# Causal products of GpSimd over two successive pairs of heads at once, with new order lists on four engines: a post-norm layer on one core

## The chip, the cores and the metric

The kernel runs on one core of a Trainium2 chip. The metric is device time in microseconds (us) of one execution. Five engines work side by side, each through its own queue in order: PE (matmul, with PEld for its weight loads), DVE (vector), ACT (activation), POOL (GpSimd) and SP (which issues the transfers). They meet only at semaphores.

## The reference, cut to what matters

For each of 16 batches of 512 rows by 128 columns: causal attention with 16 heads of 8 columns (q and k normalised, scores capped by tanh), a layer norm, then a routed block: a router picks 63 rows of each batch, which go through an attention and a feed-forward of their own and are scattered back, then a second layer norm.

```python
    def _L0_attn_ref(x, w_q, w_k, w_v, w_o):
        ...
        scores = jnp.einsum('bhqd,bhkd->bhqk', q, k) / jnp.sqrt(jnp.float32(dk))
        scores = jnp.tanh(scores / SOFTCAP) * SOFTCAP
        causal = jnp.tril(jnp.ones((S, S), dtype=bool))
        scores = jnp.where(causal[None, None], scores, -jnp.inf)
        probs = jax.nn.softmax(scores, axis=-1)
        y = jnp.einsum('bhqk,bhkd->bhqd', probs, v)
        ...
    x = L0_attn_x
    x = _layernorm(x + _L0_attn_ref(x, ...), axis=-1)
    x = _layernorm(x + _L0_ffn_ref(x, ...), axis=-1)
```

## The kernel before, in words

**The attention.** Heads are worked two at a time, so a batch has eight pairs of heads (`gi` 0 to 7; `n` counts them over all batches, 128 in all). For each pair of heads PE forms the scores with the keys on the partitions, in eight blocks of 64 keys, the causal lower part only, 2304 columns in two units (L1172, `ps_s`). ACT takes the tanh of each unit (L710, `th`) and then the exp of all 2304 columns (L725, `pr`). On the diagonal of each of the eight blocks 64 columns have to be multiplied by the triangle `tri`: `causal` on POOL (L621) does that in two instructions for each pair of heads, five blocks (320 elements a partition) and three (192). `pr` has five buffers of 2304 columns, from the 48th pair of heads on six (`probs_at`). PE's steps pv.0 to pv.3 then multiply four pairs of heads by the values (L1189), pv.4 to pv.7 the other four; the first of each four waits for the semaphore `masked`.

**The stages of a batch.** "prep" makes q, k and v (transposes, `qk0`, `qk1`, `v` on PE; the squares `sq` on POOL, sums and an inverse root on DVE, then `hi` on DVE and `lo` on POOL, L635, which split q and k into two 16-bit parts). "fin" takes the attention's output through its projection (`wo`, `res`), the layer norm (`ln`, `root1`, `root2`) and `x1`. "route" finds the chosen rows: `xw` on POOL, `w`, `row`, four comparisons `win` (L936, `wins`), `rank`, `coef`. Then, for two batches together, "sel" gathers the chosen rows and their mask (`xs`, `ss`, roots, `hn`, `hnT`, `qkv`, `qkT`, `R`, `RT`, `msel`), "att" is the routed block (`S0`, `S1` on PE, `sc0`, `mx0`, `sc1`, `mx1`, `den`, `PT0`, `PT1`, `o`, `oT`, `x1f`, roots, `h`, `hh`, `hp`, `hu`, `g`), and "late" scatters back (`proc`, `z0`, `z1`, POOL's `z_base`) and does the last layer norm (`ln`, `root1`, `root2`, `norm`). Steps called `root1` and `root2` are three or four DVE instructions each on tiny tiles (L798 to L808), an inverse root by a polynomial; moments (L883 to L893) are bn_stats and five small steps.

**What sets the order.** Four tables written out by hand: `PE_ORDER`, `VE_ORDER` (DVE), `POOL_ORDER` and `ACT_ORDER`; SP has a fixed list. An iteration `p` takes two batches (0 and 1) through 16 steps of two halves; in each half an engine runs the entries of its table, `name/k@shift`, where k is the batch of the two and the shift says by how many iterations the work lags. Scores, tanh, exp and the causal products stand in the loops themselves. Nothing but semaphores ties the halves of two engines to each other, so a table sets an order, not a time. `BANK` says which of two PSUM banks a step of PE uses, `BANK_READ` whose reading it must await.

Of the kernel before, what the change touches and what calls it, by code (L numbers as in the profile page):

```python
# [61 lines left out]
def moments_of(tiles, tag=""):  # L62
# [45 lines left out]
    [], ["prep.qk1/1@0", "att.S0@-2"],  # L108
    ["att.S1@-2", "pv.4/1@-1", "pv.5/1@-1", "route.thr/1@-2"], ["pv.6/1@-1", "pv.7/1@-1"],
    ["prep.v/1@0"], ["att.P0@-2", "att.P1@-2"],  # L110
    [], ["att.PV@-2"],
    [], ["fin.wo/1@-1", "att.oT@-2"],
    ["pv.0/0@0", "pv.1/0@0", "pv.2/0@0"], ["att.wo@-2", "pv.3/0@0", "prep.xT/0@1"],
    [], ["route.wrow/0@-1", "prep.qk0/0@1"],
    ["att.h2T@-2"], ["att.w1@-2"],
    ["route.won/0@-1"], ["prep.qk1/0@1", "route.wrow/1@-1"],
    ["pv.4/0@0", "pv.5/0@0"], ["pv.6/0@0", "pv.7/0@0"],
    ["route.thr/0@-1", "route.won/1@-1"], ["late.w2@-2", "prep.v/0@1"],
    [], ["sel.gather@-1", "sel.gather1@-1", "late.sc0@-2"],
    ["late.sc1@-2"], ["fin.wo/0@0"],  # L120
    ["pv.0/1@0", "pv.1/1@0", "sel.ET@-1", "pv.2/1@0"], [],
    ["sel.hnT@-1", "pv.3/1@0", "sel.R@-1", "sel.qkv@-1"],
    ["sel.R1@-1", "sel.R2@-1", "sel.qkT@-1", "sel.R3@-1", "prep.xT/1@1"],
# [4 lines left out]
    ["prep.qk0/1@0", "sel.msel@-2", "late.ln@-3", "prep.qk1/1@0"], ["att.sc0@-2"],  # L128
    ["att.mx0@-2", "att.sc1@-2", "att.mx1@-2", "fin.x1/0@-1"], ["route.coef/1@-2", "att.den@-2", "prep.v/1@0"],
    ["att.PT0@-2", "fin.yU1/1@-1", "prep.ss/1@0"], ["att.PT1@-2"],  # L130
# [1310 lines left out]
```

## Time and profile before

| | |
|---|---|
| median of 3 runs | 839.63 us (839.16 to 841.62) |
| profiled execution | 842.9 us, span 841.1 us |
| PE busy | 676.7 us, 80% of the span |
| DVE busy | 664.8 us, 79% |
| ACT busy | 555.4 us, 66% |
| POOL busy | 391.0 us, 46% |

The span is the time between the first and the last instruction of the profiled execution. A share of busy time is a mean over the whole of it: at the start ACT, later other engines have little left, and the end is a chain for the last two batches alone. So the rows below go by stretches. An instruction's duration in the trace runs from its start on the engine to its end, and may contain time in which it stands still.

### The profile page before, as it was taken

The numbers are of one execution on the slowest core, as the hardware profiler recorded it, in microseconds if no ns is written. First come the engines' busy times: TensorE is split into PE (matmuls) and PEld (weight loads), VectorE is DVE, ScalarE is ACT, GpSimd is POOL, SyncE is SP. The second block draws the span as 40 slices with busy tenths as digits, with TensorE's granted clock in tenths as the row PEclk, the third lists the DMA queues.
The fourth block names the chain that finished last, engine by engine and source line by source line (L and its number), as shares of the span: only waits on it lengthen the run. The fifth ranks groups of instructions, "written<-read, shape, count | busy, mean of one in ns | idle before, by whom it ended". The sixth has DMA issues, their size and how long they took to land.

```text
span 841.1 us, 16526 instructions
## 1 busy us (share of the span) xinstructions
PE 676.7 (80%) x6384; PEld 391.2 (47%) x6384; DVE 664.8 (79%) x1649; ACT 555.4 (66%) x403; POOL 391.0 (46%) x399
## 2 busy tenths in 40 slices
PE   3578787889898998888788988989789889973852
PEld 2334444535554455645454455545464546442432
DVE  3631849688979899879997899889988998588456
ACT  0388898978886778768784778688866888600000
POOL 5262645456554474455553464545635554421201
PEclk9557777889787977898896977897988978865855
DMA  6311203033303212130403012120303030000001
GB/s 188 63 34 43 55 23 76 2 63 115 76 2 63 64 22 56 39 63 2 76 28 63 14 37 53 45 46 2 64 26 64 1 64 27 13 1 26 0 1 50
DMA packets 97855, 36.72 MB, mean 44 GB/s; under 512 B 69090, under 2 KB 95090, under 8 KB 97778
## 3 DMA queue, kind: packets, MB, share of 16 engines
q1 hardware_dynamic: 97778, 35.67, 18.7%
q8 instruction: 51, 0.84, 0.4%
q14 instruction: 26, 0.21, 0.1%
HBM read 14.69 MB, written 4.19 MB: 22 GB/s over the span
## 4 chain that ended last, share of the span: by engine, by line
DVE 43%; PE 40%; issue 8%; ACT 6%; DMA 1%; POOL 1%; SPq 0%; DVEq 0%; ACTq 0%
PE ps_y L1189 10%; PE ps_s L1172 8%; PE ps_m L1288 4%; DVE wins L936 4%; ACT pr L725 3%; ACT th L710 2%; PE ps_a L1220 2%; DVE qn_v L844 2%; PE ps_m L1228 2%; DVE st L854 2%; DVE sel_v L803 2%; PE ps_a L1238 2%; DVE sel_v L802 2%; DVE v_aug L838 2%; PE ps_m L1389 1%
## 5 line engine op out<-in xcount | busy, mean ns | idle before, releaser
L710 ACT ACTIVATE th<-ps_s 128x1024 f32<-128x1024 f32 (+1 forms) x256 | 281.9, 1129 | 140.8 <-PE ps_s L1172 130.8
L621 POOL TENSOR_TENSOR pr<-pr,tri 128x320 f32<-128x320 f32 (+1 forms) x256 | 194.4, 781 | 190.3 <-ACT pr L725 190.2
L725 ACT ACTIVATE pr<-th 128x2304 f32<-128x2304 f32 x128 | 271.4, 2121 | 9.8 <-PE ps_y L1189 9.6
L1172 PE MATMUL ps_s<-q_st,k_st 32*64 32x192 f16 (+7 forms) x2048 | 197.4, 329 | 31.7 <-ACT th L710 24.3
L1189 PE MATMUL ps_y<-pr,v_aug 128*32 128x512 f32 (+7 forms) x2048 | 167.0, 470 | 0.7 <-POOL pr L621 0.7
L1172 PEld LDWEIGHTS ps_s<-q_st,k_st 32*64 32x64 f16 x2048 | 93.9, 117 | 124.6 <-issue 43.9
L1189 PEld LDWEIGHTS ps_y<-pr,v_aug 128*32 128x32 f32 x2048 | 62.5, 120 | 90.1 <-issue 74.3
L635 POOL TENSOR_TENSOR st<-qk,st 128x1024 f16<-128x1024 f32 x32 | 73.2, 2307 | 59.5 <-DVE st L854 59.5
L623 POOL TENSOR_TENSOR k_wide<-qkT,head_of 128x1024 f32<-128x1024 f32 x16 | 30.1, 1901 | 52.6 <-DVE qkT L1019 52.6
L936 DVE SCALAR_TENSOR_TENSOR wins<-w_wide,x,later 128x512 f16<-128x512 f32 (+1 forms) x64 | 48.1, 751 | 1.9
L623 POOL TENSOR_TENSOR z_base<-x,coef 128x512 f32<-128x512 f32 x16 | 16.6, 1040 | 55.0 <-DVE coef L960 55.0
L623 POOL TENSOR_TENSOR st<-qk 128x1024 f32<-128x1024 f32 x16 | 30.7, 1917 | 19.2 <-DVE qk L827 19.2
L692 ACT ACTIVATE pm<-pm 128x1008 f32<-128x1008 f32 x8 | 8.3, 1037 | 42.5 <-DVE pm L1033 42.5
L1288 PE MATMUL ps_m<-mask_a,E 128*64 128x512 f32 x112 | 36.0, 666 | 0.3 <-DVE y_out L1104 0.3
L862 DVE STREAM_TRANSPOSE y_u<-ps_y 128x512 f32<-128x512 f32 x32 | 22.8, 712 | 16.4 <-PE ps_y L1189 16.3
L1350 PE MATMUL ps_m<-vv,k_wide 128*128 128x32 f32 x128 | 26.1, 376 | 11.7 <-DVE k_wide L1045 11.7
L696 ACT ACTIVATE sc<-hu 128x512 f32<-128x512 f32 x8 | 5.0, 624 | 44.3 <-POOL hu L623 44.3
L838 DVE COPY v_aug<-ps_m 64x512 f32<-64x512 f32 x32 | 22.0, 686 | 14.7 <-PE ps_m L1228 14.2
L1238 PE MATMUL ps_a<-wT,yT 128*128 128x128 f32 x128 | 32.3, 431 | 0.0
L1350 PEld LDWEIGHTS ps_m<-vv,k_wide 128*128 128x128 f32 x128 | 25.3, 302 | 13.5 <-DVE k_wide L1045 13.5
L1238 PEld LDWEIGHTS ps_a<-wT,yT 128*128 128x128 f32 x128 | 27.7, 319 | 4.8 <-issue 4.0
L623 POOL TENSOR_TENSOR r<-x,rw_row 128x512 f32<-128x512 f32 x16 | 21.1, 1321 | 14.2 <-DVE x L912 14.2
(221 smaller groups left out, 1114.0 us busy)
## 6 DMA issues: line engine op xcount, KB each, us to landing
x_in<-in_L_attn_x SPq DMA_DIRECT2D x16, 256.0 KB, 3.4
x_res<-in_L_attn_x SPq DMA_DIRECT2D x16, 256.0 KB, 3.4
result<-y_out SPq DMA_DIRECT2D x16, 256.0 KB, 2.2
mask_a<-in_L_ffn_attention_mask SPq DMA_DIRECT2D x3, 1024.0 KB, 5.2
pr<-in_L_ffn_attention_mask SPq DMA_DIRECT2D x2, 1024.0 KB, 8.4
w_sb<-in_L_ffn_w SPq DMA_DIRECT2D x2, 256.0 KB
q_st<-st SPq DMA_TRANSPOSE x16, 4.5
k_st<-st SPq DMA_TRANSPOSE x16, 4.8
```

The source lines that it names most:

```text
L621: return nc.gpsimd.tensor_tensor(buf, buf, tri[:, None, :].to_broadcast([P, blocks, 64]), ALU.mult)
L623: mul = lambda out, a, b: nc.gpsimd.tensor_tensor(out, a, b, ALU.mult)
L635: pl["prep"].done(nc.gpsimd.tensor_tensor(lo_parts[s], qk_twice[s], hi_parts[s], ALU.subtract), f"lo_{part}", b)
L710: nc.scalar.activation(th[:, gi % 2, c0:c1], ps_s[:, c0:c1], ACT.Tanh, scale=1.0 / (QK_SCALE ** 2 * DH ** 0.5 * SOFTCAP))\
L725: nc.scalar.activation(pr[:, probs_at(n):probs_at(n) + GROUP], th[:, gi % 2, :], ACT.Exp, scale=SOFTCAP).then_inc(exp_done, 1)
L838: ve["prep"].done(nc.vector.tensor_copy(v_aug[rows, k].rearrange("p b n c -> p (b n) c")[:, :, 16 * s:16 * s + DH], at("prep.v", b)[rows, ...
L936: step(lambda: nc.vector.scalar_tensor_tensor(won[c], w_wide[:, P * c:], x1[:, k, c, D:D + 1], later[:, 0:n], ALU.is_le, ALU.mult, accum_o ...
L1172: last = mm(ps_s[64 * s:64 * s + 64, COL[kb]:COL[kb] + S - 64 * kb], k_st[rows, k, gi // 2, 64 * kb:64 * kb + 64], q_st[rows, k, gi // 2, ...
L1189: last = mm(ps_y[32 * j:32 * j + 32, 64 * kb:S], v_aug[:, k, kb, gi, :], pr[:, c:c + S - 64 * kb], start=(kb == 0), stop=(kb == NB - 1), s ...
L1238: last = mm(at("fin.wo", b)[:, P * c:P * c + P], yT[:, P * c:P * c + P], wT[:, 3, :], start=True, stop=True)
L1288: last = mm(at("sel.R")[SLOTS * k:SLOTS * k + SLOTS, :], E[:, c, SLOTS * k:SLOTS * k + SLOTS], (mask_b if k and q < 2 else mask_a)[:, c, : ...
L1350: last = mm(at("att.PV")[:, 32 * n:32 * n + 32], PT[:, n, :], vv[:, n, :, :].rearrange("p k c -> p (k c)"), start=True, stop=True)
```

## The change

`causal` now works on two successive pairs of heads, n and n + 1 with n even, in one instruction: an access pattern with one more dimension of two buffers. In place of four instructions (320, 192, 320, 192 elements) there are two (640 and 384). POOL does this at the odd pair of heads, after that one's exp, and counts `masked` once. PE waits for half as many counts. The four tables are laid anew, and with them the banks. In `VE_STEPS`, "hn" and "ET" of "sel" change places.

```diff
-            def causal(n, col, step, blocks):
-                buf = pr[:, probs_at(n) + col:probs_at(n) + col + step * blocks]\
-                    .rearrange("p (n c) -> p n c", c=step)[:, :, 0:64]
-                return nc.gpsimd.tensor_tensor(buf, buf, tri[:, None, :].to_broadcast([P, blocks, 64]), ALU.mult)
+            def causal(n, first, step, blocks):
+                lo, hi = sorted((probs_at(n) // GROUP, probs_at(n + 1) // GROUP))
+                buf = pr[:, 0:6 * GROUP].rearrange("p (g n c) -> p g n c", g=6, c=64)[
+                    :, lo:hi + 1:hi - lo, first:first + step * (blocks - 1) + 1:step, :]
+                return nc.gpsimd.tensor_tensor(buf, buf, tri[:, None, None, :].to_broadcast([P, 2, blocks, 64]), ALU.mult)
...
-                        pool.wait_ge(exp_done, b.no * 8 + (gi + 1))
-                        causal(b.no * 8 + gi, 0, 512, 5)
-                        causal(b.no * 8 + gi, 960, 448, 3).then_inc(masked, 1)
+                        if gi % 2:
+                            pool.wait_ge(exp_done, b.no * 8 + (gi + 1))
+                            causal(b.no * 8 + gi - 1, 0, 8, 5)
+                            causal(b.no * 8 + gi - 1, 15, 7, 3).then_inc(masked, 1)
...
-                    t_.wait_ge(masked, b.no * 8 + (4 * half + 4))
+                    t_.wait_ge(masked, b.no * 4 + (2 * half + 2))
...
-    ["sel.RT@-1"], ["prep.qk0/1@1", "sel.msel@-1"],
+    [], ["sel.RT@-1", "prep.qk0/1@1"],
```

In POOL's table the steps move too. Before, `sel.zb` (z_base) and `prep.sq/1` stood in the first half of an iteration and `route.xw/0` in the eighth; now the three follow each other in the third. `att.kw` (k_wide) now comes directly behind `prep.lo/0`; before, two pairs of heads stood between. In the changed file the lines of these parts stand one or two lower.

On DVE, in the middle of the program, behind the two casts of prep.hi for an even batch (`st<-qk`; `sel_v` is the tile of sel.root1, `y_out<-ps_m` is late.z1, `hnT` sel.hnT). Before:

```order
L854 CAST st<-qk 128x64x16
L854 CAST st<-qk 128x128x8
L800 TENSOR_SCALAR sel_v<-sel_v 128x1
L802 TENSOR_TENSOR sel_v<-sel_v 128x1
L803 TENSOR_TENSOR sel_v<-sel_v 128x1
L805 SCALAR_TENSOR_TENSOR sel_v<-sel_v 128x1
```

After:

```order
L855 CAST st<-qk 128x64x16
L855 CAST st<-qk 128x128x8
L1105 TENSOR_TENSOR y_out<-ps_m,z_base 128x512
L979 COPY ET<-ps_a 128x512
L995 TENSOR_SCALAR hnT<-ps_m,g 128x256
L884 BN_STATS stats<-y_out 128x6 x8
L887 TENSOR_TENSOR mv<-stats 128x8
```

sel.root1 and sel.root2 now stand ahead of the casts; late.z1 and late.ln have come behind them.

On DVE, behind the two casts of prep.hi for an odd batch (`x<-r` is route.w, `r<-ps_a` fin.res; `w_wide` is route.row). Before:

```order
L854 CAST st<-qk 128x64x16
L854 CAST st<-qk 128x128x8
L920 TENSOR_REDUCE x<-r 128x4
L921 TENSOR_SCALAR x<-x,rb 128x4
L901 TENSOR_TENSOR r<-ps_a,x_res 128x512
```

After:

```order
L855 CAST st<-qk 128x64x16
L855 CAST st<-qk 128x128x8
L930 COPY w_wide<-ps_a 128x512
L878 STREAM_TRANSPOSE yT<-y_n 128x512
L1059 COPY oT<-ps_m 128x128
L937 SCALAR_TENSOR_TENSOR wins,cnt<-w_wide,x,later 128x512
```

route.row and route.win of the even batch now follow the casts, and route.w stands earlier.

On DVE, from the copy of R (`w_wide<-ps_m`) to att.sc0 (`sc`). Before:

```order
L980 COPY w_wide<-ps_m 128x512
L822 COPY xT<-ps_a 128x512
L992 COPY RT<-ps_m 128x512
L805 SCALAR_TENSOR_TENSOR ln_v<-ln_v 128x4
L806 SCALAR_TENSOR_TENSOR ln_v<-ln_v 128x4
L807 SCALAR_TENSOR_TENSOR ln_v<-ln_v 128x4
L808 SCALAR_TENSOR_TENSOR ln_v<-ln_v 128x4
L827 COPY qk<-ps_a 128x8x64
L1018 COPY msel<-ps_m 128x64
L883 BN_STATS stats<-y_out 128x6 x8
L886 TENSOR_TENSOR mv<-stats 128x8
```

After:

```order
L981 COPY w_wide<-ps_m 128x512
L823 COPY xT<-ps_a 128x512
L863 STREAM_TRANSPOSE y_u<-ps_y 128x512
L993 COPY RT<-ps_a 128x512
L828 COPY qk<-ps_m 128x8x64
L1019 COPY msel<-ps_a 128x64
L1027 SCALAR_TENSOR_TENSOR sc<-ps_m,msel 128x512
L1033 TENSOR_REDUCE mx<-sc 128x8
L1034 TENSOR_TENSOR pm<-sc,mx 128x8x63
L828 COPY qk<-ps_m 128x8x64
```

att.sc0 now follows msel at once; fin.root2 and late.ln, which stood between the copy of RT and att.sc0, are elsewhere, and qk1/1 has moved behind att.mx0. On PE the same place reads, after the change (`w_wide` transposed is RT, `wT,xT` is qk0/1, `E,RT` is msel, `k_wide,qkT` is S0):

```order
L1197 MATMUL ps_a<-ident,w_wide 128x128 x4
L1221 MATMUL ps_m<-wT,xT 128x8x32 x2
L1173 MATMUL ps_s<-q_st,k_st 64x512 x2
L1173 MATMUL ps_s<-q_st,k_st 64x448 x2
L1173 MATMUL ps_s<-q_st,k_st 64x64 x2
L1321 MATMUL ps_a<-E,RT 64x64 x8
L1337 MATMUL ps_m<-k_wide,qkT 64x512 x2
```

Before, S0 stood behind another unit of scores and qk1/1; msel came directly behind qk0/1.

## Rows read from the trace of the kernel before

**Rows 1.** Busy time of each engine by stretch, then clock, DMA share, GB/s.

```profile
40.00:196.80 156.80, 130.34 (x1278) 66.70 (x1277) 97.90 (x199) 134.81 (x97) 80.77 (x81) 0.75 0.24 54
473.90:563.90 90.00, 80.06 (x801) 46.32 (x801) 82.68 (x204) 69.02 (x52) 47.83 (x47) 0.85 0.19 42
196.80:742.00 545.20, 478.23 (x4716) 276.60 (x4714) 481.06 (x1187) 410.07 (x297) 280.53 (x274) 0.84 0.18 39
742.00:841.10 99.10, 51.37 (x306) 36.97 (x298) 66.23 (x220) 3.35 (x4) 13.74 (x11) 0.62 0.06 17
```

**Rows 2.** DVE's waits, 473.9 to 563.9 us: first and last of seven; total, times, longest.

```profile
DVE r L901 <- PE ps_a L1238: 1.1, 1, 1.1
...
DVE w_wide L929 <- PE ps_m L1196: 0.3, 1, 0.3
```

**Rows 3.** Timeline, 540.3 to 547.5 us: start, duration, instruction.

```profile
541.17 4.60 POOL L635 TENSOR_TENSOR st<-qk,st 128x1024 f16<-128x1024 f32 x2 [5.15 <-DVE st L854]
...
541.79 1.90 DVE L802 TENSOR_TENSOR sel_v<-sel_v 128x1 f32<-128x1 f32 x1
...
543.73 2.05 DVE L803 TENSOR_TENSOR sel_v<-sel_v 128x1 f32<-128x1 f32 x1
```

**Rows 4.** Single lines over the whole run: shortest, median, longest in ns.

```profile
L802 DVE TENSOR_TENSOR sel_v<-sel_v x16: 158/360/1909, 174.8 to 814.8; 128x1 f32<-128x1 f32 x16
L870 DVE TENSOR_TENSOR y_n<-y_u,rd x16: 691/774/1877, 87.8 to 749.6; 128x512 f32<-128x512 f32 x16
L886 DVE TENSOR_TENSOR mv<-stats x24: 164/348/1200, 98.6 to 834.0; 128x4 f32<-128x4 f32 x16, 128x8 f32<-128x8 f32 x8
L921 DVE TENSOR_SCALAR x<-x,rb x16: 231/517/1391, 136.2 to 766.7; 128x4 f32<-128x4 f32 x16
```

**Rows 5.** Timeline of DVE: the first, one and the last of the long ones.

```profile
488.60 0.86 DVE L870 TENSOR_TENSOR y_n<-y_u,rd 128x512 f32<-128x512 f32 x1
...
498.48 1.38 DVE L921 TENSOR_SCALAR x<-x,rb 128x4 f32<-128x4 f32 x1
...
563.27 0.99 DVE L886 TENSOR_TENSOR mv<-stats 128x8 f32<-128x8 f32 x1
```

**Rows 6.** Groups by form, whole run: busy us, mean ns, idle before.

```profile
L621 POOL TENSOR_TENSOR pr<-pr,tri 128x320 f32<-128x320 f32 x128 | 115.4, 902 | 190.3 <-ACT pr L725 190.2
...
L621 POOL TENSOR_TENSOR pr<-pr,tri 128x192 f32<-128x192 f32 x128 | 84.4, 660 | 0.0
```

**Rows 7.** Groups by form of POOL, 473.9 to 563.9 us.

```profile
L635 POOL TENSOR_TENSOR st<-qk,st 128x1024 f16<-128x1024 f32 x4 | 9.2, 2319 | 8.6 <-DVE st L854 8.6
L623 POOL TENSOR_TENSOR st<-qk 128x1024 f32<-128x1024 f32 x2 | 3.8, 1892 | 0.0
...
L623 POOL TENSOR_TENSOR z_base<-x,coef 128x512 f32<-128x512 f32 x3 | 3.1, 1041 | 7.2 <-DVE coef L960 7.2
...
L623 POOL TENSOR_TENSOR sc<-hb 128x512 f32<-128x512 f32 x1 | 1.0, 1039 | 2.0 <-DVE hb L1081 2.0
```

**Rows 8.** Groups by form of DVE, 473.9 to 563.9 us.

```profile
L844 DVE TENSOR_REDUCE qn_v<-st 128x128 f32<-128x1024 f32 x2 | 2.4, 1196 | 0.0
...
L883 DVE BATCH_NORM_STATS2 stats<-y_out 128x6 f32<-128x128 f32 x8 | 1.6, 276 | 0.0
...
L978 DVE COPY ET<-ps_a 128x512 f32<-128x512 f32 x1 | 0.7, 691 | 0.0
```

**Rows 9.** Timeline of PE, 554.5 to 566.7 us.

```profile
558.38 1.13 PE L1220 MATMUL ps_a<-wT,xT 128*128 128x256 f32 x4
559.44 0.97 PE L1320 MATMUL ps_m<-E,RT 128*64 128x64 f32 x16
...
562.86 1.08 PE L1336 MATMUL ps_a<-k_wide,qkT 128*64 128x512 f32 x4
563.87 0.62 PE L1172 MATMUL ps_s<-q_st,k_st 32*64 32x512 f16 x6
```

**Rows 10.** ACT's waits, 40 to 200 us: total, times, longest.

```profile
ACT pr L725 <- PE ps_y L1189: 5.5, 5, 1.6
```

More of the change, by code:

```diff
@@ L107 @@
 PE_ORDER = (
[L108 to L123, printed above, removed]
-    ["sel.RT@-1"], ["prep.qk0/1@1", "sel.msel@-1"],
+    ["sel.msel@-2", "att.S0@-2"], ["att.S1@-2", "prep.qk1/1@0"],
+    ["pv.4/1@-1", "pv.5/1@-1", "route.thr/1@-2"], ["pv.6/1@-1", "pv.7/1@-1", "prep.v/1@0"],
@@ L125 @@
+    ["late.sc0@-2", "late.sc1@-2"], ["sel.ET@-1", "pv.0/1@0", "pv.1/1@0"],
+    ["pv.2/1@0", "pv.3/1@0", "sel.hnT@-1"], ["sel.R@-1", "sel.qkv@-1"],
+    [], ["sel.R1@-1", "sel.R2@-1", "sel.qkT@-1", "sel.R3@-1", "prep.xT/1@1"],
+    [], ["sel.RT@-1", "prep.qk0/1@1"],
 )
 VE_ORDER = (
[L128 to L130 removed]
@@ L138 @@
-    ["route.row/1@-1"], ["prep.qk1/0@1", "route.win/1@-1"],
-    ["late.norm@-3", "att.g@-2", "route.coef/0@-1"], ["route.rank/1@-1", "fin.yU1/0@0"],
-    ["prep.v/0@1", "late.proc@-2", "fin.y/0@0"],
-    ["prep.ss/0@1", "prep.root1/0@1", "fin.yT/0@0", "sel.xs@-1", "late.z0@-2"],
-    ["prep.root2/0@1", "sel.ss@-1", "prep.qkn/0@1"], ["fin.res/0@0", "prep.hi/0@1", "sel.root1@-1"],
-    ["sel.root2@-1", "sel.ET@-1"], ["sel.hn@-1", "late.z1@-2"],
-    ["sel.hnT@-1", "fin.ln/0@0", "fin.yU0/1@0", "sel.qkv@-1", "fin.root1/0@0"], ["sel.qkT@-1", "sel.R@-1"],
@@ new lines @@
+    ["prep.qk0/0@1"], ["att.hn@-2", "late.root1@-3", "fin.x1/1@-1", "att.h2T@-2"],
+    ["route.coef/0@-1", "fin.yU0/0@0", "route.w/1@-1"],
+    ["att.h@-2", "late.root2@-3", "att.hp@-2", "route.row/1@-1", "route.win/1@-1", "late.norm@-3", "att.g@-2", "prep.qk1/0@1"],
+    ["prep.v/0@1", "fin.yU1/0@0", "late.proc@-2", "route.rank/1@-1"], ["fin.y/0@0", "fin.yT/0@0", "sel.xs@-1"],
+    ["sel.ss@-1", "sel.root1@-1"], ["prep.ss/0@1", "fin.res/0@0", "late.z0@-2", "prep.root1/0@1", "prep.root2/0@1"],
@@ L146 @@
+    ["sel.root2@-1", "prep.qkn/0@1"], ["sel.hn@-1"],
+    [], ["prep.hi/0@1", "late.z1@-2", "sel.ET@-1"],
+    ["sel.hnT@-1", "late.ln@-2", "sel.qkv@-1"], ["fin.ln/0@0"],
+    [], ["sel.qkT@-1", "sel.R@-1"],
+    ["prep.xT/1@1", "fin.yU0/1@0", "sel.RT@-1"], ["prep.qk0/1@1", "sel.msel@-1", "att.sc0@-1"],
+    ["att.mx0@-1", "prep.qk1/1@1"], ["att.sc1@-1", "fin.root1/0@0", "att.mx1@-1"],
 )
 POOL_ORDER = (
-    ["sel.zb@-2", "prep.sq/1@0"], [],
+    [], [],
+    ["sel.zb@-2", "prep.sq/1@0", "route.xw/0@-1"], [],
@@ L251 @@
[L251 to L261 removed]
+    "att.PV": ["att.PT0@0"],
+    "att.S0": ["prep.qk0/1@2", "sel.R@0"],
```

134 lines of the change are left out of this document (70 added, 64 removed), and 2 rows, old and new, of the table VE_STEPS.

## The prediction

> **What bounds the kernel now.** I read the busy time by stretch first [rows 1]. From 196.8 to 742 us the batches flow through in pairs, six pairs in 545.2 us, of 92 us each but for the last; call one such turn a period. In the period from 473.9 to 563.9 DVE is busy 82.7 of 90.0 us, PE 80.1, ACT 69.0, POOL 47.8. The table of waits for the same period says which of the two full engines waits for which: DVE waits seven times, 4.0 us together [rows 2]; the rest of its 7.3 us without work is gaps between one instruction and the next. So DVE sets the pace here, and a microsecond more or less in its queue is a microsecond of the period. The stretch before (40 to 196.8) is another kind: ACT is busy 134.8 of 156.8 us, DVE 97.9. In the tail (742 to 841.1) nothing is full: it is one chain of dependent steps.
>
> The reader is to see next that DVE's busy time is not all work. At 541.17 POOL begins the two subtractions of prep.lo, 4.60 us; DVE's multiplications of a single element then take 1.90 and 2.05 us and end as POOL's two instructions do [rows 3]. The same form takes 0.16 us when it is quick [rows 4]. I went through the period and set each DVE instruction that starts under a running POOL instruction against the shortest of its own form and size: 29 are longer by over 0.06 us, 16.6 us together, from y_n at 488.60 (0.86 for 0.69) to the first moment step at 563.27 (0.99 for 0.16) [rows 4, 5]. Twenty of them stand behind causal products, 8.0 us (4.7 behind the wide ones, 3.3 behind the narrow ones, sixteen of each); nine behind other POOL work, 8.6 us, of which prep.lo alone makes 5.0. The 29 have two inputs in SBUF or are tensor_scalar steps from SBUF to SBUF; copies out of PSUM, transposes, reductions and bn_stats are never among them. Below, "open" steps are those of the 29's kinds.
>
> The Trainium skill says this in "SBUF — State Buffer", section "Who interferes with whom": VectorE and GpSimd share one port pair, which is an exclusive lock for a whole instruction, and DVE wants it for an instruction with two SBUF inputs and for some single-input forms. The trace agrees, at 1.90 us for one element.
>
> **The change, part by part.**
>
> *The products.* A period has 16 pairs of instructions, 0.90 us (320 elements) and 0.66 us (192) on the mean [rows 6]. The straight line through both is 0.30 us plus 1.89 ns an element, so 640 elements take 1.51 and 384 take 1.02. Eight times 2.53 us is 20.3 against sixteen times 1.56, 25.0. If nothing of the 0.30 is fixed it stays 25.0. POOL itself has over 42 us to spare in a period, so its saving is worth nothing by itself; what counts is how long DVE stands behind it. Today a product of 0.90 us costs DVE 4.7/16 = 0.295 us and one of 0.66 costs 3.3/16 = 0.205. On that line (0.37 us more per us of product) the merged ones cost 0.52 and 0.34, eight times that is 6.9 us, 1.1 less than now. If every additional us is waited out (DVE has an open step ready all the while), they cost 0.90 and 0.42, 10.5 us, 2.5 more than now. I take 0.2 less: nearer to the measured line, but not on it, since DVE comes to an open step the more surely the longer a product goes on. Bounds: -1.1 and +2.5.
>
> The page's rule by itself speaks against the merge: the loser is blocked to the end of the instruction, so an instruction twice as long blocks longer. By its worst case the sum would be the +2.5.
>
> *What DVE does behind the other POOL work.* This is the larger term, and the order lists decide it. Lengths of POOL work from [rows 7], of cover from [rows 8].
> - After prep.hi of the even batch DVE now goes to three quick copies and the eight bn_stats of late.ln, instead of sel.root1. prep.lo lasts 2 x 2.32 = 4.6 us from the end of hi_q. Cover: hi_k 0.6, z1 and ET 0.69 each, hnT some 0.5, bn_stats 1.6, together 4.1. Left: 0.5, against 3.64 now (1.90 + 2.05 - 2 x 0.16).
> - After prep.hi of the odd batch: copy and transpose of 0.69 each, oT some 0.3, then route.win, which is open. Cover with hi_k 2.2 of 4.6, left 2.4, against 1.34 now (L921 1.38 for 0.23 [rows 4, 5], and a first moment step 0.19). This one gets worse.
> - After route.coef/1 POOL does z_base twice (2.1), the squares (1.9) and xw/0 (1.0 to 1.4): 5.0 to 5.4 us. DVE has den and ss (1.2 each) and four copies (2.8): 5.2. Left about 0; now z_base and an xw cost 0.82 and 0.88.
> - xw/1 no longer falls on route.win: some 0.5, now 0.79. k_wide is covered by copies: 0, now 0.80. hh now meets late.root2 at once: 1.0, now 0.28; hu then meets win/1: 0.6, now 0.
>
> Together 5.0 us for 8.6: -3.6. The bounds are -5 (all covered) and -1 (the odd batch's loss stays, half of the rest comes back as POOL's queue shifts).
>
> *New waits of DVE for PE.* PE's steps have moved too. DVE now goes from the copy of RT through qk0/1 and msel straight to att.sc0; before, late.ln and qk1/1 stood between. PE meanwhile has qk0/1 (1.13), half a score group (0.62), msel (0.97) and S0 (1.08) [rows 9]. Laid out from the moment at which DVE starts to copy R, each DVE copy at 0.6 from start to start: DVE copies R, xT, y_u and RT until 2.4; PE has transposed RT by 1.3, is through qk0/1 at 2.4, the scores at 3.1, msel at 4.0, S0 at 5.1, then half a score group, S1 and qk1/1 until 8.2. DVE is ready for msel at 3.1, for sc0 at 4.2 and, after sc0, mx0 and sub0, for qk1/1 at 7.3: waits of 1.0, 1.1 and 0.9, together 3.0. The present waits in this region (qkT, R, RT) are 1.6 of the 4.0 [rows 2]; two of them get cover from fin.ln/0 and yU0/1. Others laid out in the same way: den and PT1 0.7, res/1 0.5, xs 0.7 (the gather is behind rank/1 with only y/0 and yT/0 between), h, proc and rank/0 0.3 each. Sum 5.8 against 4.0: +1.8. Bounds 0 (PE is ahead) and +5.6 (the four steps run at the lower clock level, 3.8 us more; the granted clock of the period is 0.85).
>
> *The mask later.* The first of a pair now waits for the second exp, and the pair's last product ends about 2.5 us after that exp, not 1.56. PE's pv waits for it, and exp waits for pv where five buffers are all there are. In the stretch where ACT is full, exp has waited five times, 5.5 us [rows 10]: up to 1.0 us is added to each, and to three more halves perhaps. I take +4 (bounds 0 and +8). Later ACT has 21 us a period to spare and it costs nothing; without that cover it would be 4 us a period.
>
> *The tail.* late.ln of the last pair but one moves ahead, behind qkv's round trip to PE, instead of standing in front of att.sc0 of the last pair: 2.5 us off the chain, of which I take 2 (bounds 0 and 4).
>
> **Sum.** A period: -3.6 - 0.2 + 1.8 = -2.0. 545.2 us hold 5.9 periods: -11.8. With +4 and -2: -9.8 us. The profiled execution took 842.9 us (span 841.1 and 1.8 around it), which gives 833.1; it is 3.3 over the median of the runs, 839.6, which gives 829.8. I say 830.
>
> **Rivals.**
> - *Larger gain.* Waits stay at 4.0 and the products follow the line: -4.7 a period, -27.7, with the ends -25.7: 814 us. For it: PE has 10 us a period free. Against: the ladder from RT to sc0 is a true dependency.
> - *No change.* Waits eat what the lock gives back: within 0.3%, 837 to 842 (0.3% is about what a measurement of this kernel can tell).
> - *Longer hold, slower.* The merged products each stop a chain of small two-input steps (roots, moments, win) for their whole length: +2.5 in place of -0.2, a period +0.7, in all +6: 846. It decides from the point where DVE stands 9.5 us a period behind products, not 8.0 (-3.6 + 1.5 + 1.8, and the +2 of the two ends spread over 5.9 periods). This is the page's rule as a result of its own; for it, the chain at 541 us, where two long instructions were waited out nearly whole; against it, the line of today's two lengths.
> - *The ladder, slower.* PE's four steps late or at the lower clock: +5.6 in place of +1.8, a period +1.8, in all +13: 852. It decides from 3.5 us more waits a period.
>
> **Chances.** Forecast (3 to 15 us gained) 0.38, larger gain 0.20, no change 0.13, longer hold 0.15, ladder 0.14. So faster 0.58, same 0.13, slower 0.29. The range takes in the larger gain a little beyond its time and the ladder: 808 to 853. Cases of both signs hold much of the chance; the forecast's own range is 824 to 837.
>
> **What would show it.** Right: periods of about 90 us; single-element steps of sel.root1 at 0.16 us throughout; products of about 1.5 and 1.0 us; DVE still busy over 85% with waits of 5 to 6 us a period, the largest before msel, sc0 and qk1/1; the first win of the odd batch long. Wrong: products of 1.8 us and more; small two-input steps of 1 to 1.5 us in rows behind the products; DVE's waits for S0 or msel over 2 us each; or exp waiting for pv past 200 us.

## The result, and the profile after

The changed kernel takes 809.57 us (median of four runs, 798.82 to 812.37) against 839.57 before; the medians stand at 0.964. The 95% interval of the ratio, 0.9467 to 0.9664 around 0.9566, is taken over the two runs within 1.5% of the fastest, 798.82 and 808.17. The forecast was 830: the sign is right and the median lies in the range of 808 to 853, near its lower end, but the gain is 30 us and not 10. The profiled run took 810.97 us; a later series of the same kernel gave 806.64 to 808.21 (median 807.20, against 838.54 before), so I read its profile as the usual case.

The busy time by stretch, of the kernel after; the stretches answer to those of [rows 1]: ACT-full start, one full period, the middle, the tail.

```profile
41.70:203.20 161.50, 130.38 (x1280) 65.38 (x1280) 93.06 (x194) 134.77 (x98) 72.05 (x48) 0.81 0.23 52
452.90:535.80 82.90, 72.89 (x799) 42.64 (x798) 73.17 (x204) 68.93 (x52) 44.64 (x32) 0.92 0.22 46
203.20:713.00 509.80, 454.60 (x4713) 261.96 (x4712) 431.72 (x1192) 409.57 (x297) 260.48 (x179) 0.87 0.20 42
713.00:809.10 96.10, 48.24 (x302) 35.52 (x298) 65.25 (x221) 3.35 (x4) 13.77 (x11) 0.64 0.06 17
```

Set against [rows 1], DVE has 9.5 us less in a period for the same 204 instructions, PE 7.2 less for two instructions fewer, and the granted clock is 0.92 where it was 0.85 (0.88 for 0.85 on the mean of four full periods). The start is 4.7 us longer, the tail 3.0 shorter. The chain of work that ended last went through DVE first in the kernel before; in the kernel after PE leads. Before, then after:

```profile
DVE 43%; PE 40%; issue 8%; ACT 6%; DMA 1%; POOL 1%; SPq 0%; DVEq 0%; ACTq 0%
PE 47%; DVE 26%; issue 11%; POOL 7%; ACT 6%; DMA 2%; SPq 0%; DVEq 0%; ACTq 0%; POOLq 0%
```

From one first exp of 16 heads to the next the starts are, before: 40.0, 116.2, 196.8, 286.2, 379.4, 473.9, 563.9, 655.4, last exp 731.8; after: 41.7, 120.9, 203.2, 286.0, 370.9, 452.9, 535.8, 623.0, last exp 702.8. By stretch:

| stretch | before | after | difference | forecast |
|---|---|---|---|---|
| up to the first exp | 40.0 | 41.7 | +1.7 | - |
| first 32 heads | 156.8 | 161.5 | +4.7 | +4 |
| five periods | 458.6 | 419.8 | -38.8 | -2.0 each |
| last 16 heads | 76.4 | 79.8 | +3.4 | a period's -2.0 |
| tail | 109.3 | 106.2 | -3.1 | -2 |

So the surprise lies in the five periods: -38.8 us where -10 was forecast. The last 16 heads went the other way, +3.4 for -2.0; no run looked at why. I took each DVE step there that starts under a running POOL instruction against the shortest of its form, as in the prediction, and summed the excess, over the four periods with the same 203 to 204 DVE instructions (before from 286.2 us, after from 286.0 us):

| mean of four periods, us | before | after |
|---|---|---|
| length | 92.3 | 84.2 |
| DVE's loss behind products | 7.9 | 2.4 |
| DVE's loss behind other POOL work | 9.4 | 4.9 |
| DVE's gaps of 0.15 us and more | 5.9 | 7.1 |

The two one-element steps of sel.root1 that [rows 3] shows, by source line (shortest, median, longest in ns):

```profile
L803 DVE TENSOR_TENSOR sel_v<-sel_v x16: 159/159/161, 177.6 to 782.9; 128x1 f32<-128x1 f32 x16
L804 DVE TENSOR_TENSOR sel_v<-sel_v x16: 159/159/1528, 177.8 to 783.1; 128x1 f32<-128x1 f32 x16
```

The merged products, by form over the whole run:

```profile
L621 POOL TENSOR_TENSOR pr<-pr,tri 128x640 f32<-128x640 f32 x64 | 98.9, 1545 | 122.5 <-ACT pr L726 122.5
L621 POOL TENSOR_TENSOR pr<-pr,tri 128x384 f32<-128x384 f32 x64 | 67.3, 1051 | 0.0
```

POOL and DVE on the timeline where prep.lo of the even batch runs:

```profile
518.73 4.61 POOL L635 TENSOR_TENSOR st<-qk,st 128x1024 f16<-128x1024 f32 x2 [5.22 <-DVE st L855]
520.76 1.64 DVE L884 BATCH_NORM_STATS2 stats<-y_out 128x6 f32<-128x128 f32 x8
522.43 0.93 DVE L887 TENSOR_TENSOR mv<-stats 128x8 f32<-128x8 f32 x1
```

The one-element step that took 1.90 us under prep.lo [rows 3, 4] now takes 0.16 us in all sixteen cases, and the one behind it, which took 2.05, in fifteen of sixteen (once, at 593.97 us, it took 1.53 behind a merged product). What is left of that hold falls on one moment step, 0.93 for 0.17 us, as costed (0.76 for 0.5). The merged products take 1.55 and 1.05 us, as worked out from [rows 6] (1.51, 1.02).

DVE's waits in the full period, to set beside [rows 2] (total, times, longest):

```profile
DVE r L902 <- PE ps_m L1239: 1.2, 1, 1.2
DVE RT L993 <- PE ps_a L1197: 1.0, 1, 1.0
DVE msel L1019 <- PE ps_a L1321: 0.8, 1, 0.8
...
DVE sc L1027 <- PE ps_m L1337: 0.6, 1, 0.6
```

With the smaller ones it is 6.0 us; the forecast said 5.8. The sum is met partly by luck: msel, att.sc0 and qk1/1 (0.2) make 1.6 us where 3.0 was costed, fin.res (the first row) 1.2 where 0.5 was, and RT's 1.0 had no term of its own.

### The profile page after: what moved, and what is told of

It is laid out like the page before. It is cut to its first block, busy times and chain, and to the rows that moved or that the text cites. A ratio compares the mean times of both kernels' runs of the same rounds, so it can differ in the third digit from the quotient of the medians.

```text
span 809.1 us, 16395 instructions
## 1 busy us (share of the span) xinstructions
PE 651.0 (80%) x6384; PEld 374.3 (46%) x6384; DVE 609.7 (75%) x1649; ACT 554.9 (69%) x403; POOL 362.3 (45%) x271
## 4 chain that ended last, share of the span: by engine, by line
PE 47%; DVE 26%; issue 11%; POOL 7%; ACT 6%; DMA 2%; SPq 0%; DVEq 0%; ACTq 0%; POOLq 0%
PE ps_y L1190 17%; PE ps_s L1173 10%; POOL pr L621 4%; ACT pr L726 4%; PE ps_a L1197 3%; PE ps_m L1239 2%; POOL k_wide L623 2%; ACT th L711 2%; DMA k_st<-st 2%; PE ps_m L1229 2%; PE ps_m L1289 2%; DVE stats L884 2%; PE ps_m L1374 2%; PE ps_a L1221 1%; DVE y_out L1116 1%
## 5 line engine op out<-in xcount | busy, mean ns | idle before, releaser
L1173 PE MATMUL ps_s<-q_st,k_st 32*64 32x512 f16 (+7 forms) x2048 | 196.6, 324 | 39.6 <-ACT th L711 32.2
L621 POOL TENSOR_TENSOR pr<-pr,tri 128x640 f32<-128x640 f32 (+1 forms) x128 | 163.3, 1298 | 122.5 <-ACT pr L726 122.5
L1190 PE MATMUL ps_y<-pr,v_aug 128*32 128x512 f32 (+7 forms) x2048 | 164.4, 466 | 8.7 <-POOL pr L621 8.6
L635 POOL TENSOR_TENSOR st<-qk,st 128x1024 f16<-128x1024 f32 x32 | 76.5, 2408 | 48.3 <-DVE st L855 48.3
L937 DVE SCALAR_TENSOR_TENSOR wins<-w_wide,x,later 128x512 f16<-128x512 f32 (+1 forms) x64 | 53.7, 838 | 2.6
L828 DVE COPY qk<-ps_a 128x512 f32<-128x512 f32 x16 | 11.0, 690 | 40.0 <-PE ps_a L1221 40.0
L1289 PE MATMUL ps_m<-mask_a,E 128*64 128x512 f32 x112 | 32.7, 611 | 0.6 <-DVE hnT L995 0.6
L839 DVE COPY v_aug<-ps_m 64x512 f32<-64x512 f32 x32 | 21.7, 677 | 13.8 <-PE ps_m L1229 13.3
L1239 PE MATMUL ps_m<-wT,yT 128*128 128x128 f32 x128 | 21.1, 315 | 9.3 <-DVE xs L977 5.4
L1239 PEld LDWEIGHTS ps_m<-wT,yT 128*128 128x128 f32 x128 | 17.9, 216 | 11.8 <-DVE yT L878 9.8
L828 DVE COPY qk<-ps_m 128x512 f32<-128x512 f32 x16 | 11.0, 690 | 16.2 <-PE ps_m L1221 16.1
L863 DVE STREAM_TRANSPOSE y_u<-ps_y 128x512 f32<-128x512 f32 x32 | 22.6, 708 | 0.2
```

The source lines that it names most:

```text
L621: return nc.gpsimd.tensor_tensor(buf, buf, tri[:, None, None, :].to_broadcast([P, 2, blocks, 64]), ALU.mult)
L635: pl["prep"].done(nc.gpsimd.tensor_tensor(lo_parts[s], qk_twice[s], hi_parts[s], ALU.subtract), f"lo_{part}", b)
L863: ve["fin"].done(nc.vector.transpose(y_u[:, half], ps_y[:, :]), f"yU{half}", b)
L937: step(lambda: nc.vector.scalar_tensor_tensor(won[c], w_wide[:, P * c:], x1[:, k, c, D:D + 1], later[:, 0:n], ALU.is_le, ALU.mult, accum_o ...
L1173: last = mm(ps_s[64 * s:64 * s + 64, COL[kb]:COL[kb] + S - 64 * kb], k_st[rows, k, gi // 2, 64 * kb:64 * kb + 64], q_st[rows, k, gi // 2, ...
L1190: last = mm(ps_y[32 * j:32 * j + 32, 64 * kb:S], v_aug[:, k, kb, gi, :], pr[:, c:c + S - 64 * kb], start=(kb == 0), stop=(kb == NB - 1), s ...
```

## The experiments

All times are medians beside runs of the kernel before on the same chip, which took 837.7 to 839.0 us. The "four corners" below are the old and the new lists, each with single and with merged products. My first theory (A) was that the new lists put the products beside DVE steps that they don't stop; its rivals, that the merge itself spares DVE (B) or holds it longer (C). What these runs left over gave theory E: part of the gain is PE's clock.

**Each half alone.** The first run has the new order lists and the old single products; the second has the old lists and the merged products. The core of the first, against the changed kernel (the second is the same edit, the other way round, in the kernel before):

```diff
-                        if gi % 2:
-                            pool.wait_ge(exp_done, b.no * 8 + (gi + 1))
...
-                            causal(b.no * 8 + gi - 1, 0, 8, 5)
-                            causal(b.no * 8 + gi - 1, 15, 7, 3).then_inc(masked, 1)
+                        pool.wait_ge(exp_done, b.no * 8 + (gi + 1))
...
+                        causal(b.no * 8 + gi, 0, 512, 5)
+                        causal(b.no * 8 + gi, 960, 448, 3).then_inc(masked, 1)
```

> The new order lists with the old products: two instructions for each pair of heads, masked counted eight times a batch. Theory A (the new lists put the products beside DVE steps that they don't stop): DVE stands some 2 to 3 us a period behind products as in the changed kernel, and the time is 800 to 815. Theory B (the merge itself spares DVE, since it is stopped half as often): the loss behind products goes back to some 8 us a period, six periods of +5.8: 835 to 845. Theory C (a longer hold stops DVE longer, the lists alone gain more): under 800.

> The old order lists with the merged products. Theory A: the loss behind products follows their length, 6.9 to 10.5 us a period for 8.0, prep.lo still costs 5.0: 833 to 855, no clear change. Theory B: loss behind products down to some 2 us a period, 805 to 815. Theory C: 10.5 us or more, 855 and over.

Measured: the lists alone 837.92 us, ratio 0.9997 [0.9978, 1.0016]; the merge alone 856.37 us, 1.021 [1.0178, 1.0242]. Neither gains; both together gain 30. For the lists alone the loss behind products (3.9 us in the table below) is nearer to theory A's and the time is theory B's; for the merge alone theory C holds, in loss and in time. The mean of four periods, worked out as in the table above:

| us | before | lists alone | merge alone | both |
|---|---|---|---|---|
| length | 92.3 | 92.2 | 93.6 | 84.2 |
| loss behind products | 7.9 | 3.9 | 11.4 | 2.4 |
| loss behind other POOL work | 9.4 | 4.8 | 7.3 | 4.9 |
| DVE's gaps of 0.15 us and more | 5.9 | 13.3 | 6.0 | 7.1 |

The same merge adds 3.5 us a period to DVE's loss under the old lists and takes 1.5 off under the new ones. What differs is seen on one pair of steps of route.rank, `E` and `edge`. In the kernel before, and then with the merge alone, they start under a pair of products:

```profile
515.46 1.59 POOL L621 TENSOR_TENSOR pr<-pr,tri 128x320 f32<-128x320 f32 x2
515.69 0.91 DVE L947 TENSOR_TENSOR E<-rank,slot_no 128x256 f32<-128x256 f32 x1
516.71 0.36 DVE L951 SCALAR_TENSOR_TENSOR edge<-rank,x 128x4 f32<-128x4 f32 x1
...
524.62 2.67 POOL L622 TENSOR_TENSOR pr<-pr,tri 128x640 f32<-128x640 f32 x2
524.85 1.58 DVE L949 TENSOR_TENSOR E<-rank,slot_no 128x256 f32<-128x256 f32 x1
526.55 0.77 DVE L953 SCALAR_TENSOR_TENSOR edge<-rank,x 128x4 f32<-128x4 f32 x1
```

In the changed kernel's timeline the pair of products is over before they come:

```profile
503.97 2.50 POOL L621 TENSOR_TENSOR pr<-pr,tri 128x640 f32<-128x640 f32 x2
506.73 0.42 DVE L948 TENSOR_TENSOR E<-rank,slot_no 128x256 f32<-128x256 f32 x1
507.26 0.17 DVE L952 SCALAR_TENSOR_TENSOR edge<-rank,x 128x4 f32<-128x4 f32 x1
```

The two places in the period where this pair runs cost 1.44 us before (excess over 0.42 and 0.17), 3.6 with the merge alone and nothing in this period of the changed kernel (0.56 in the next, where `E` starts under a product again). The Trainium skill ("SBUF — State Buffer", section "Who interferes with whom") says that the loser of the shared port is blocked for the winner's whole instruction. The merge alone agrees: with the longer instructions the loss is 11.4 us for 7.9. The changed kernel, with 2.4 us behind the same long instructions, shows that only steps which come while the instruction runs pay for its length.

**Without the products.** Each product is cut to one or two elements, so the diagonal of the causal mask is left out; all instructions, waits and signals stay. Changed kernel, kernel before, and new lists with single products.

```diff
-                    :, lo:hi + 1:hi - lo, first:first + step * (blocks - 1) + 1:step, :]
+                    :, lo:hi + 1:hi - lo, first:first + 1, 0:1]
```

> The changed kernel with each causal product cut to two elements (the mask on the diagonal blocks is left out). It shows what is still lost behind products there. Theory A: 2.1 us a period behind products, 6 periods, and up to 1 us at each of some eight waits of exp in the first stretch: 790 to 800. If the merged products cost nothing that DVE shows: 805 to 812.

> The kernel before with each causal product cut to one element (the mask on the diagonal blocks is left out). If DVE's time behind products (8.0 us a period, 58 in all) is time of the period one for one: 790 to 800. If PE, busy 80 of 90 us, takes over at once: 815 to 830.

> New order lists, single products (16 blocks of two a period, one signal a head), each cut to one element: the diagonal mask is left out. The run with the new lists and whole single products took 837.9 us, the changed kernel with its products cut 785.1 us. Theory A (the time that the products hold GpSimd and the shared access is what costs): the count of instructions and signals does not matter, so this run is at 783 to 790 us. Theory D (with single products the signal for each head and the number of instructions itself hold something up, whatever their length): at least 800 us. Theory A puts the whole 50 us between this run and the lists alone on the length of the products.

Measured: 785.09, 799.7 and 784.5 us. The number of instructions and signals is worth nothing (785.1 and 784.5). With products so short the lists give 14.6 us. The length of the products costs 38.5 us under the old lists, 53.4 with single products under the new ones, and 24.5 merged under the new ones. That is all that the length does, pv's later start included, and not DVE's loss alone. From old to new, the gain is thus 14.6 us of lists and 14.0 us of cheaper products. (The changed kernel came out under its range here, which began at 790.) One full period of the changed kernel without products, in which PE is the busiest engine:

```profile
360.70:442.50 81.80, 76.32 (x799) 44.17 (x798) 71.02 (x204) 68.98 (x52) 26.37 (x30) 0.87 0.23 47
```

And one of the kernel before without them, PE again the busiest:

```profile
364.40:449.10 84.70, 78.68 (x801) 45.82 (x797) 75.45 (x204) 68.97 (x52) 29.14 (x46) 0.86 0.22 45
```

**Why the lists alone gain nothing.** They take DVE's loss from 17.3 to 8.7 us a period, and the period stays at 92.2. DVE's waits for PE in it, with the lists alone:

```profile
DVE xs L975 <- PE ps_m L1273: 2.8, 1, 2.8
DVE y_out L1103 <- PE ps_a L1388: 2.3, 1, 2.3
DVE hnT L993 <- PE ps_m L1301: 2.1, 1, 2.1
DVE r L900 <- PE ps_m L1237: 1.8, 2, 1.6
```

The first two, late.proc's 1.5 us and some half a microsecond more, 7.0 us in all, lie in one stretch, the middle one of this view of the lists alone (the columns are those of [rows 1]). The wait for hnT ends at 544.0, just behind it; the longer one of fin.res, 1.6 us, ends at 497.1, ahead of it, and is not new (1.2 in the changed kernel).

```profile
466.40:519.70 53.30, 44.65 (x508) 25.35 (x506) 48.90 (x128) 44.32 (x34) 30.26 (x30) 0.84 0.18 41
519.70:540.20 20.50, 19.73 (x116) 14.51 (x116) 12.46 (x36) 10.09 (x7) 4.93 (x7) 0.50 0.05 14
540.20:558.50 18.30, 18.30 (x183) 9.19 (x176) 13.37 (x42) 14.60 (x11) 12.54 (x11) 1.00 0.44 73
```

In the changed kernel's period the same work, in the second of these stretches, runs at full clock; the third row is the same part of its next period.

```profile
452.90:505.00 52.10, 44.06 (x514) 25.56 (x513) 47.51 (x129) 44.15 (x34) 27.82 (x21) 0.87 0.19 42
505.00:535.80 30.80, 28.83 (x288) 17.08 (x287) 25.66 (x75) 24.79 (x19) 16.82 (x12) 1.00 0.29 53
...
588.00:623.00 35.00, 33.44 (x288) 19.44 (x288) 26.71 (x76) 24.67 (x18) 17.44 (x12) 0.85 0.23 39
```

A granted clock of 0.50 is 1.2 GHz. The changed kernel's next period has such a stretch too, 10.2 us of it, and the part with the same 288 matmuls takes 4.2 us more. Two low stretches per period, some 15 to 25 and 35 to 45 us behind its start, are in the profiles of all four corners; this third one is in every full period of the lists alone (20.4 us) and in one of four of the changed kernel (the kernel before and the merge alone have one of 7 to 10 us in each). On PE's timeline of the lists alone it begins about a short wait for DVE's v_aug:

```profile
519.97 2.04 PE L1379 MATMUL ps_m<-w_sb,hu 128*128 128x128 f32 x8 [0.94 <-DVE v_aug L837]
521.95 2.12 PE L1171 MATMUL ps_s<-q_st,k_st 32*64 32x512 f16 x16
```

The same place in the changed kernel, at full clock:

```profile
504.33 1.13 PE L1381 MATMUL ps_m<-w_sb,hu 128*128 128x128 f32 x8 [0.58 <-DVE v_aug L839]
505.39 1.17 PE L1173 MATMUL ps_s<-q_st,k_st 32*64 32x512 f16 x16
```

In the changed kernel's next period, the one with a third stretch, the wait at this place is 0.74 us; the stretch begins 7.8 us behind it, at 595.2, after PE has waited 1.12 us for xs.

To test whether the low clock is what the lists alone lose, I gave PE matmuls to do ahead of its waits for DVE; nothing reads their results. In all these runs the wait for the PSUM bank also moves ahead of the wait for DVE at the four steps named below.

```diff
+            def fill(bank):
+                for _ in range(3):
+                    mm(bank[:, 256:512], ident[:, :], wT[:, 0:2, :].rearrange("p a d -> p (a d)"), start=True, stop=True)
...
-                ve["att"].wait(t_, q, "g")
...
+                fill(at("late.w2"))
+                ve["att"].wait(t_, q, "g")
```

First ahead of four steps of PE: att.oT (attention out), att.h2T (the transposed row ahead of the feed-forward), late.w2 (its second weight), once a period each, and route.won (the routing row), twice. This was done with the lists alone, in the changed kernel and in the kernel before:

> The new lists with single products (837.9 us), and three extra matmuls of 128x256, whose results nothing reads, ahead of each of four waits of TensorE for VectorE in every batch (attention out, transposed FFN hidden, second FFN weight, routing row). Theory E (what keeps the lists alone slow is not VectorE's loss, 8.7 us a period, but TensorE at its low clock behind these waits, 519.7 to 540.2 us of the profile): the low stretches of 37.6 us a period shrink under 20 us, the period falls from 92.1 toward 83 to 86 us and the time to 795 to 815 us. Theory A (the loss under the products alone decides): the clock may rise, but the time stays within 1% of 838 us, or rises by the extra matmuls, up to 3 us a period (858 us).

> The changed kernel with the same extra matmuls. Theory E: the low stretches of 14 to 27 us a period shrink, and the runs, which lay between 798.8 and 812.4 us, come out at or under 799 us. Theory A: no gain, 800 to 812 us, since VectorE at 73 of 83 us a period has no room to give; the extra matmuls may cost up to 2 us a period (823 us).

> The kernel before with the extra matmuls at all four places. If the low clock costs under the old lists what it costs under the new ones with single products: 815 to 825 us. If under the old lists VectorE sets the end (16.6 us of loss a period, busy 80 of 90 us), the clock rises and the time does not fall: 835 to 850 us. The forecast held the second.

Then at route.won and late.w2 alone, with the lists alone and in the changed kernel; and six at att.oT alone in the changed kernel:

> The new lists with single products (837.9 us), with the extra matmuls at two of the four places only: three ahead of the routing row and three ahead of the second FFN weight, in every batch. In the profile of the lists alone TensorE waits 0.7 and 0.9 us there, its granted clock falls to 0.5 right after (20 us a period, 53 to 74 us behind the period's start), and VectorE's waits for TensorE lie in that stretch; the changed kernel has the first two low stretches of the period too, but not this one. Theory E (this one low stretch is what the lists alone lose): it goes, the period falls from 92.2 to 82 to 86 us, and the time to 795 to 818 us, below the run with the matmuls at four places (821.7). Rival (the waits move elsewhere, and the place does not matter): 825 us or more.

> The changed kernel with the extra matmuls at the same two places. Its profile has no low stretch there, so theory E expects no gain: 800 to 815 us, and at most 3 us from the run with single products above if the merge is worth little once the clock is the same (theory A: the merge takes 1.3 us a period off VectorE's loss under the products, which would be 8 us in all).

> The changed kernel with six extra matmuls a batch ahead of TensorE's longest wait alone (2.8 us, attention out), where they cost no time that TensorE would use. Theory E: the low stretch around this wait (16 to 23 us behind the period's start) shrinks, 790 to 803 us. Rival (work in this stretch is not on the path that sets the end): 803 to 815 us, as without them.

And at route.won and late.w2 with one matmul for three:

> The new lists with single products and the extra matmuls at the two places (routing row, second FFN weight), one at each instead of three: about 1.6 us of TensorE a period instead of 4.7. Theory E (the third low stretch is what the lists alone lose, and what was left of the time with three was the matmuls themselves): the stretch is gone or shorter than 10 us, the period 84 to 86.5 us, 808 to 822 us. Rival (one is too little to change anything, or the time with three came from something else): 825 to 840 us.

> The changed kernel with one extra matmul at each of the two places. Its periods mostly have no third low stretch, so theory E expects no gain but a smaller cost than with three (819.8): 806 to 814 us. A version below 805 us would be better than the changed kernel.

Measured (us, medians):

| extra matmuls | lists alone | changed | before |
|---|---|---|---|
| none | 837.9 | 809.6 | 838 to 839 |
| 3 at four steps | 821.65 | 817.1 | 868.7 |
| 3 at two steps | 825.2 | 819.8 | - |
| 6 at one step | - | 824.7 | - |
| 1 at two steps | 815.3 | 809.7 | - |

The lightest one decides. One extra matmul ahead of each of three steps a period, 2.1 us of PE, takes 22.6 us off the lists alone (815.3, expected 808 to 822), and the third stretch is gone from all four full periods, which take 85.6 us on the mean. One of them up to the place where the stretch would begin, and the 22.5 us from there:

```profile
371.40:423.50 52.10, 45.51 (x487) 25.18 (x487) 47.57 (x126) 42.46 (x32) 29.58 (x30) 0.80 0.17 38
423.50:446.00 22.50, 21.61 (x245) 14.49 (x242) 19.78 (x57) 16.72 (x13) 10.94 (x9) 1.00 0.19 43
```

PE's timeline at the place (L1210 is the extra work):

```profile
425.34 0.67 PE L1210 MATMUL ps_m<-wT,ident 128*128 128x256 f32 x2
425.85 1.05 PE L1385 MATMUL ps_m<-w_sb,hu 128*128 128x128 f32 x8
```

The eight matmuls that took 2.04 us take 1.05. DVE's gaps fall to 5.7 us a period (mean of four) and its loss stays high, 9.8, of which 4.4 behind products. In the changed kernel the same edit is worth nothing (809.73, expected 806 to 814). It doesn't hold the clock there: two of the four full periods of its profile have a third stretch, of 6.8 us, and are longer by some 5 us. One with and one without:

```profile
288.00:375.60 87.60, 78.82 (x805) 46.03 (x804) 74.25 (x204) 68.99 (x52) 43.85 (x31) 0.86 0.21 43
375.60:457.40 81.80, 74.24 (x805) 43.80 (x804) 72.05 (x204) 68.91 (x51) 43.59 (x30) 0.92 0.21 47
```

The heavier runs were sized badly. I had allowed up to 2 or 3 us a period for the extra matmuls; those at four steps take 9.1 us a period in the trace of the lists alone and those at two steps 4.7, so both times mix what the matmuls mend and what they cost. At four steps the lists alone (821.65) lie between the ranges of theory and rival, at two steps (825.2) just in the rival's. The changed kernel missed theory E's ranges both times (799 or less at four steps, 800 to 815 at two) and att.oT's 824.7 both sides'. At att.oT the expectation that they cost nothing was wrong. They write to the bank of the step itself, so they begin only when DVE has copied xT out of it, run at the low clock (0.50 from 480.0 to 486.8), and hold the transpose behind them until 486.98, where att.oT's input was there at 482.84 (482.27 and 0.57 of DVE):

```profile
481.87 5.28 PE L1212 MATMUL ps_m<-wT,ident 128*128 128x256 f32 x12 [1.69 <-DVE xT L823]
486.98 0.27 PE L1363 MATMUL ps_m<-ident,o_tm 128*128 128x128 f32 x1
```

In the kernel before they cost 30 us, more than either side expected. DVE's loss rises to 20 us a period there, and what share of the 30 is which I have not taken apart.

**One placement undone.** The changed kernel with sel.root2 and sel.hn behind prep.hi again, so that they meet prep.lo:

```diff
-    ["sel.root2@-1", "prep.qkn/0@1"], ["sel.hn@-1"],
-    [], ["prep.hi/0@1", "late.z1@-2", "sel.ET@-1"],
+    ["prep.qkn/0@1"], [],
+    [], ["prep.hi/0@1", "sel.root2@-1", "sel.hn@-1", "late.z1@-2", "sel.ET@-1"],
```

> The changed kernel with two VectorE steps (the second root step of the selection and its normalized row) put back behind the first input conversion, where they stand in the kernel before; all else as changed. Theory A by the prediction's term for this place (3.2 us a period over 5.9 periods and the first stretch): 825 to 832 us. Rival (the steps moved alone are worth little, and slack of VectorE, 10 us a period, takes the hold): 805 to 815 us.

Measured: 838.71 us, 1.0007 [0.9988, 1.0025]: this one move takes the whole gain back. The two steps wait out prep.lo again:

```profile
550.20 4.60 POOL L635 TENSOR_TENSOR st<-qk,st 128x1024 f16<-128x1024 f32 x2 [6.77 <-DVE st L855]
...
550.63 2.09 DVE L806 SCALAR_TENSOR_TENSOR sel_v<-sel_v 128x1 f32<-128x1 f32 x1
552.76 2.06 DVE L807 SCALAR_TENSOR_TENSOR sel_v<-sel_v 128x1 f32<-128x1 f32 x1
```

DVE's loss rises by 3.6 us a period (10.9 for 7.3, mean of four), 3.1 of it behind other POOL work than the products; the prediction had costed the place at 3.1. The periods rise by 5.0 (89.3 on the mean), and each of them now has a third low stretch of 7 to 10 us. So the loss is right, and the time is more than the loss; the expectation, which made the time from the loss, missed by 7 us. The move also puts hn, which PE waits for, behind the hold; what share that has is not shown.

**One microsecond more.** Two extra DVE sums (0.67 us each, 1.27 for the two since they overlap) a period, once ahead of the gate step, once ahead of late.z1, and the changed kernel itself beside them. The edit ahead of the gate step:

```diff
+                for i in range(2):
+                    nc.vector.tensor_reduce(extra[:, i:i + 1], hq[:, :], AX.X, ALU.add)
                 ve["att"].done(nc.vector.scalar_tensor_tensor(hu[:, :], hq[:, :], 1.0, hb[:, :], ALU.add, ALU.mult), "g", q)
```

> The changed kernel with two extra VectorE steps a period (sums over 512 elements, whose results nothing reads; about 0.55 us each, 1.1 us in all) right ahead of the gate step, after which TensorE waits for VectorE before the second FFN weight. Theory E (a little more lateness of VectorE here lets TensorE fall to 1.2 GHz for 10 to 20 us of the period, as in one of four full periods of the changed kernel and in all four of the lists alone): a third low stretch (53 to 80 us behind the period's start) in at least three of four full periods, the period 87 to 92 us, the time 830 to 848 us. Rival (lateness adds up one to one): 1.1 us over seven periods, 8 us: 815 to 821 us.

> The changed kernel with the same two extra steps behind the place: ahead of the second score row of the late stage, from which the period's last third runs with TensorE at full clock. Theory E: no more low stretches than in the changed kernel, since VectorE waits up to 1 us for TensorE later in this part; 803 to 820 us, and below the run with the steps ahead of the place by at least 10 us. Rival (one to one): 815 to 821 us, the same as there.

> The changed kernel itself, unaltered, on the chip of these two runs: 798 to 813 us as before, for the comparison with them. Theory E: what tells its runs apart is how many periods have a third low stretch, so the profile of a run near 800 us has it in none of the full periods, one near 810 us in one or two.

Measured: 818.97, 813.12 and 807.2 us. Ahead of the place the steps cost 11.8 us, little more than one to one over eight turns of 1.27 us; a third stretch of only 3.4 us appears in three of four periods. So my theory that a microsecond of lateness there brings the long stretch is refuted. Behind the place they cost 5.9 us, not 10 less than ahead of it as expected, and bring a stretch of 10.2 us into every other period (one with, one without):

```profile
286.90:374.40 87.50, 78.84 (x799) 45.70 (x798) 75.31 (x206) 68.99 (x52) 44.06 (x31) 0.84 0.22 43
374.40:457.40 83.00, 74.35 (x799) 43.18 (x798) 72.97 (x206) 68.98 (x52) 44.06 (x31) 0.90 0.22 46
```

The control (profiled at 808.21 us) has no third stretch in its four full periods, where theory E put that at 800 us, and no run near 800 us either, so the one run of 798.82 us stays without an explanation.

## Why the prediction was wrong

**Right, by its own steps.** DVE's loss under POOL was the place to look. The other POOL work: 9.4 to 4.9 us a period where 8.6 to 5.0 was forecast, with prep.lo of the even batch at 0.76 (0.5 costed), route.win of the odd batch the one that gets worse (2.37 us for one instruction of 384 elements, 1.75 over its shortest, and 0.37 on the one ahead of it; 2.4 costed), route.coef 0.49, late.root2 behind hh 0.80 (1.0 costed). DVE's waits: 6.0 listed for 5.8, in part by luck. The tail: -3.1 for -2. The mask later: +4.7 in the first 32 heads for +4, though not where I put it; exp's waits for pv hardly rose, and tanh waits for the scores (in the kernel before 13.5 us in the same view):

```profile
ACT th L711 <- PE ps_s L1173: 17.6, 9, 2.8
ACT pr L726 <- PE ps_y L1190: 6.3, 5, 1.3
```

Without products the two kernels differ by 14.6 us; the terms of the sum apart from products and mask make 12.6 (5.9 times 1.8, and 2).

**The step that failed is the products' term.** It laid what a product costs DVE in the kernel before on the merged ones and came to -0.2 us a period. Measured: 7.9 to 2.4, -5.5. The other terms of a period came within a microsecond each (loss behind other POOL work -4.5 for -3.6, DVE's gaps +1.2 for +1.8), so this one makes most of the miss, -8.1 us a period for -2.0. The cost of a product belongs to the old order and its timing. It says how often one of the blocked kinds of step happened to come up while a product ran, and the lists were changed together with the products. The lists alone make -4.0 of it with the old single products, and the merge -1.5 more on top. Even under one order it is no constant: 2.0, 2.0, 2.3 and 3.3 us in the four periods of the changed kernel. I had gone through every POOL instruction against the new DVE list but for the products, which are half of POOL's time. The runs without products say the same in time: products and mask were to cost 2.8 us together (5.9 times -0.2, and 4), and the products' length costs 14.0 us less (24.5 for 38.5).

"Longer hold" was a rival with the right mechanism for the wrong order, and its bound holds a slip. If all the additional time is waited out, a narrow product costs 0.205 + 0.36, 0.57 us and not 0.42, so the bound is 11.8 us a period and not 10.5. Under the old lists the loss went to 11.4, close to it, and the time up by 18 us. (The "seven times" that DVE waits in the prediction are seven rows with eight waits.)

**A second step failed with it:** that a microsecond in DVE's queue is a microsecond of the period. The lists alone spare DVE 8.6 us a period and gain nothing, because PE then runs a stretch of 20 us at 1.2 GHz and DVE waits in it and just behind it; three light matmuls a period bring out 22.6 us. The prediction named PE's clock only as a price in the ladder rival (3.8 us for four steps at the lower level) and had no term for how the clock itself changes with the order: 0.85 to 0.88 over the four full periods. That the time still lies in the range is luck: the lower end was there for "larger gain" (814 us), whose mechanism, waits of 4.0 us and products on the line of the old ones (-1.1), is not what happened.

**What the merge is worth.** Under the new lists without extra matmuls it seems to be worth 28 us, under the old ones it costs 18. With extra matmuls the single products stand 5.6 us above the merged ones in the lightest pair, 4.5 and 5.4 in the two heavier ones. Only the pair at four steps has no third stretch in any full period of either kernel (4.5 us); in the other two the changed kernel has one in two of four, so those differences also hold some clock. The lists with the light matmuls stand 22.7 us under the kernel before without them; that edit was not tried in the kernel before, so how much of the 22.7 is the order alone is open.

**Open.** What begins the third stretch is not settled. With the lists alone it starts behind idle times of PE, 0.7 and 0.9 us, at route.won and late.w2, and extra work there removes it. In the changed kernel it starts some 6 us later in the period, the wait at late.w2 is 0.58 us in a period without it and 0.74 in the one with it, and the same extra work doesn't remove it; 1.3 us more of DVE ahead of late.w2 gave only a short one. No version that leaves nothing of the mask out beat the changed kernel.
